# A gated delta-rule layer on one core: two position changes in hand-written engine orders

## What is computed

```python
mixed_qkv = einsum('bsh,ch->bcs', x, Wqkv)          # 2048 q + 2048 k + 4096 v channels
mixed_qkv = silu(causal_depthwise_conv(mixed_qkv, conv_w))   # 4 taps
beta, g = sigmoid(b), -exp(A_log) * softplus(a + dt_bias)
for t in time:                                       # per head, state 128 x 128
    state = state * exp(g_t)
    delta = (v_t - state^T k_t) * beta_t
    state = state + k_t delta^T
    out_t = state^T q_t                              # q, k are l2-normalised
y = (rms_norm(out) * norm_w * silu(z)) @ Wout.T
```

## Time and profile before

| | |
|---|---|
| median of 3 runs | 3998.91 us (3998.87 to 4000.12) |
| the profiled execution's own time | 3996.14 us |
| its span on the core | 3994.4 us |
| mean granted TensorE clock | 0.954 of full speed |
| busy share PE / DVE / ACT / POOL | 87% / 72% / 50% / 23% |
| turns of the delta stage | 64, some 40.4 to 42.8 us each |

### The profile page before, as it was taken

How to read it: one execution, slowest core, us unless ns; L and a number is a source line. 1 busy time by engine, 2 the same in 40 slices (tenths; PEclk the granted TensorE clock), 3 DMA queues, 4 the chain that set the end, 5 groups by cost and what they waited for, 6 DMA issues and landing times. The chain is left out here.

```text
span 3994.4 us, 82462 instructions
## 1 busy us (share of the span) xinstructions
PE 3462.2 (87%) x29419; PEld 2470.9 (62%) x29438; DVE 2876.2 (72%) x5136; ACT 2000.5 (50%) x4971; POOL 927.0 (23%) x1273
## 2 busy tenths in 40 slices
PE   7999977725899999999999999999999999995185
PEld 6888855414566666666666666666666666663142
DVE  3444459984777777777777777777777777775897
ACT  2233320024565666656666565666656666564354
POOL 0000034302223232222323223232232323230000
PEclk9999989867999999999999999999999999997598
DMA  2000021101011000010100101001010110101201
GB/s 100 12 12 6 12 86 34 29 13 53 22 28 34 22 29 23 28 39 17 34 18 28 39 17 34 18 29 38 17 34 18 33 34 17 34 17 43 84 1 43
DMA packets 44453, 122.64 MB, mean 31 GB/s; under 512 B 5872, under 2 KB 11120, under 8 KB 40688
## 3 DMA queue, kind: packets, MB, share of 16 engines
q1 hardware_dynamic: 44016, 116.87, 9.1%
HBM read 112.32 MB, written 4.54 MB: 29 GB/s over the span
## 5 line engine op out<-in xcount | busy, mean ns | idle before, releaser
L1838 DVE SCALAR_TENSOR_TENSOR delta_F<-delta_bank,delta_cw,delta_F 128x510 f32<-128x510 f32 (+2 forms) x768 | 571.4, 744 | 113.4 <-ACT delta_F L1656 94.3
L1846 DVE TENSOR_TENSOR delta_Pb<-delta_bank,delta_lev 128x512 f16<-128x512 f32 x448 | 312.7, 698 | 261.5 <-PE delta_bank L2159 247.4
L2133 PE MATMUL delta_bank<-delta_xh,delta_qkvh 128*128 128x512 f16 x1024 | 391.1, 382 | 20.6 <-DVE delta_F L1838 15.4
L1656 ACT ACTIVATE delta_F<-delta_bank,delta_cw 128x512 f32<-128x512 f32 x256 | 175.9, 687 | 445.9 <-PE delta_bank L2133 445.9
L2133 PE MATMUL delta_bank<-delta_xl,delta_qkvh 128*128 128x512 f16 x1024 | 390.9, 382 | 0.0
L2133 PE MATMUL delta_bank<-delta_xh,delta_qkvl 128*128 128x512 f16 x1024 | 390.2, 381 | 0.0
L1855 DVE CAST delta_XT<-delta_bank 128x512 f16<-128x512 f32 x448 | 309.6, 691 | 43.9 <-PE delta_bank L2182 43.6
L1626 ACT ACTIVATE delta_Xi<-delta_bank 128x512 f16<-128x512 f32 x320 | 190.5, 595 | 192.2 <-PE delta_bank L2178 192.2
L2118 PE MATMUL delta_bank<-delta_zh,delta_xh 128*128 128x256 f16 x1024 | 280.5, 274 | 5.0 <-ACT delta_gz L1678 0.6
L1464 POOL TENSOR_SCALAR_AFFINE_SELECT delta_LA<-delta_LA 128x512 f32<-128x512 f32 x128 | 81.6, 637 | 863.1 <-DVE delta_LA L1866 720.8
L2118 PE MATMUL delta_bank<-delta_zl,delta_xh 128*128 128x256 f16 x1024 | 279.7, 273 | 0.0
(11 more groups left out here) (304 smaller groups left out, 9200.5 us busy)
## 6 DMA issues: line engine op xcount, KB each, us to landing
delta_Gb<-g_rows SPq DMA_DIRECT2D x66, 512.0 KB, 5.2
delta_st_qkv<-in_Wqkv SPq DMA_DIRECT2D x17, 1024.0 KB, 8.4
delta_st_z<-in_Wz SPq DMA_DIRECT2D x17, 512.0 KB, 6.1
conv_T<-filters SPq DMA_DIRECT2D x32, 256.0 KB, 3.1
delta_st_o<-in_Wout SPq DMA_DIRECT2D x16, 512.0 KB, 8.1
ffn_ahead_W<-in_W SPq DMA_DIRECT2D x2, 4096.0 KB, 17.4
conv_ahead_C<-in_ctx_rev SPq DMA_DIRECT2D x1, 6144.0 KB, 17.5
attn_xt<-in_xT SPq DMA_DIRECT2D x10, 512.0 KB, 3.9
```

The source lines that it names most:

```text
L1656: sc.activation(F[:, i, :], bank[AT[job] % 2][:, :], ACT.Copy, scale=cw_tap(i, 3))\
L1838: ve.scalar_tensor_tensor(dst, src, cw_tap(i, 3 - lag), dst, ALU.mult, ALU.add)\
L1846: ve.tensor_tensor(left(Pb[:, lvl, :, :], lvl), comp(bank[5], lvl), bc(lev[:, lvl, :].rearrange("p (n s) -> p n s", s=1 << lvl), 1, 8), AL ...
L2133: ins = te.matmul(bk[:, :], ww[:, QKV[job], kc, :], xx[:, kc, tok:tok + 512], start=(m == 0), stop=(m == 11))
```

## The change

Two edits, both in order only. No instruction is added, removed or altered, and no wait is added or removed. On DVE the two splits of the output weight move down, the first behind `decayed_j0(1)`, the second behind `newton`. On PE `values_token_major(1)` moves from ahead of `fill(5)` to behind it.

```diff
@@ DVE's order @@
                 output_variance()
                 level_xt(4, 0)
                 add_out(3, -2)
-                next_o(0)
-                next_o(1)
                 level_p(5, 0)
                 decayed_j0(1)
+                next_o(0)
                 newton()
+                next_o(1)
                 conv_lag("q", 1, 2, 3)
                 level_xt(5, 0)
                 level_p(6, 0)
@@ PE's order @@
                 level_a(6, 0)
                 fill(4)
                 level_b(6, 0)
+                fill(5)
                 values_token_major(1)
-                fill(5)
                 level_a(0, 1)
                 answer(0, 0)
                 transpose_out(0)
```

## The result

The changed kernel takes 4016.34 us (median of 5 runs, 4015.12 to 4022.99), the kernel before 3998.87 on the same chip (5 runs). The ratio is 1.0049, with a 95% interval of 1.0035 to 1.0063: slower by some 0.5%. The profiled execution took 4015.24 us, 19.1 more than the one before; the medians are 17.5 apart.

What follows compares the result with a forecast made beforehand. The prediction took PE to bound the delta stage, with DVE setting the pace from level_a(5) to z0.0. Four turns cost 3 x 0.34 + 0.20 - 0.09 = 1.13 us, times 15.5 is 17.5: median 4016, range 4003 to 4028.

Steps and rivals of the forecast that it cites:

- z0.0 is pinned behind `conv_lag("k")`: On PE, z0.0 waits for DVE's conv_lag("k") and starts 0.06 to 0.13 us behind its end, whatever PE did before.
- the new wait: PE's idle time gathers at z0.0 as one wait, some 62 times 1.5 us, near 90 us.
- The PE edit costs 0.34 us in three turns and 0.20 in one: times_L(0, 0) on PE starts later behind z0.0: 0.34 us in three turns of four, 0.20 in the other.
- the issue wait: Idle of 0.15 us before the answer in one turn of four; its slack takes 0.14 of the delay, leaving 0.20.
- the transposes': Second pair of value transposes on PE, now behind z0.1: take 0.49 us, so level_a(0) starts 0.49 later.
- ACT's path: conv_tap("v0") to first_answer(0): level with PE's path; if the longer, 0.40 us in place of 0.34, 4 us more in all.
- The DVE edit gains 0.09 us in a split turn: In 16 turns level_p(5) starts 1.42 us earlier, the splits' 1.33 come back before conv_lag("q"): 0.09 gained, between nothing and 0.2.
- Sum: Both edits over four turns: 3 x 0.34 + 0.20 - 0.09 = 1.13 us; 15.5 such groups make 17.5 us.
- the 0.79 wait was the only one: Rival at PE's transposes: level_a(0) comes 0.79 us earlier in each of 62 turns, -49 us, 3950; chance 0.05.
- the delay is taken up later: Rival: slack between times_L and level_a(5) absorbs the delay, no change, 3991 to 4007; chance 0.13.
- The upper bound: Rival: the answer keeps its 0.41 us behind level_a(0), costing 0.49 in all turns, 30 us, 4029; chance 0.08.
- The clock: Rival: long idle before z0.0 lowers PE's clock, 1.5 us each turn, 91 us in all, about 4107; chance 0.02.

Runs made afterwards that it cites:

- out_early: Kernel before, with transpose_out(0) moved on PE from behind the answer to ahead of values_token_major(1): ratio 0.9937.
- z_behind_answer: Kernel before plus the PE edit, with room moved from fill(5) to fill(6) so z0.0 and z0.1 come behind the answer: ratio 1.0028.
- splits_behind_newton: Kernel before, PE's order unchanged, with both output-weight splits moved on DVE behind newton: ratio 1.0017.

## Why the prediction was right, and where it wasn't

The forecast of 4016 met the measured 4016.34, but closer than its terms deserve. Two of them were off, in opposite directions, and the profiled execution grew by 19.1 us, not by the forecast's 17.5; that the medians stand just 17.5 apart is luck within their scatter of several us.

- *z0.0 is pinned behind `conv_lag("k")`.* Right: 0.06 to 0.13 us behind it in all 62 turns of both kernels, and the new wait came as named (62 times, 93.5 us, for "near 90").
- *The PE edit costs 0.34 us in three turns and 0.20 in one.* The mechanism held, the size was high. `times_L` starts 3.77 behind z0.0 in all four kinds of turn now; before, it was 3.51 in two, 3.70 in the kind of the earlier trace rows and 3.44 in the kind ahead of a split turn. So the edit cost 0.27 twice, 0.07 where the issue wait vanished as supposed, and 0.33 in the last kind, which I had not told apart: there z0.0 stands 0.13 behind `conv_lag("k")`, and the answer, which waited for the cast and not for z0.0, stood only 0.57 behind z0.0. Four turns cost 0.94 instead of 1.22. The term that was mis-sized is the transposes': I took 0.49 us from their old place, and behind z0.1 they take 0.43 to 0.44 and are recorded with 0.60 instead of 0.66. Why is open. The missing idle time alone isn't shown to be it: in `out_early` they take 0.49 with no idle time ahead (1812.20 to 1812.69). The shorter group shortens PE's path and ACT's. ACT's `conv_tap("v0")` started at 0.87, only 0.04 behind the recorded end, so the modelled end was not late by the 0.12 that would have made ACT's path the longer one. From the answer to `times_L` PE takes 2.88 us, against 2.87 before, so ACT added nothing that can be seen; with `first_answer(0)` done 0.07 before `times_L`, the two paths came out level, as forecast.
- *The DVE edit gains 0.09 us in a split turn.* Wrong in sign: it lost 0.29, and 5 us alone. The step that failed is "The splits' 1.33 us come back ahead of `conv_lag("q")`, however. What is left is 1.42 - 1.33 = 0.09 us". They came back as 1.33 plus the 0.37 by which `newton` slowed beside POOL, and 1.42 - 1.33 - 0.37 is -0.28. Its slow third operation was in the trace of before, beside POOL's select; I didn't ask what stood beside it on POOL.
- *Sum.* 0.94 + 0.29 = 1.23 us in four turns for the 1.13 of the forecast, and 15.5 times that is the 19.1 of the profiled executions. A match to the tenth is more than this sum can promise, since the issue waits at the loop's seam vary between 1.1 and 1.8 us from one pass to the next.
- *Rivals.* That the 0.79 wait was the only one is refuted by `z_behind_answer` too. That the delay is taken up later is refuted: from `times_L` to the next turn's `decayed_j1` it is 33.37 us before and 33.38 after in ordinary turns. The upper bound, 0.49 in each turn, was not reached: no kind of turn lost more than 0.33. The clock stayed where it was: the granted clock from 1000 to 3600 us is 1.00 (2.4 GHz) in both kernels, with 1.5 us of idle time in each turn.

## What to carry to other kernels

When one engine stands idle for another, follow the other's order beyond the operation that ends the wait: here three more gates stood right behind it, and reordering the waiting engine only moved the idle time and put new work behind the last gate. What helps is independent work from behind the last gate, brought into the idle time, or taking work off the other engine ahead of it. Before moving a DVE operation that has all its inputs in SBUF, look at what POOL does at the new place.

## What the runs showed of the hardware

Where a DVE operation with its inputs in SBUF alone met a POOL operation, one of the two took longer. A split of 128x512 took 0.74 to 0.75 us with POOL idle, 1.18 beside POOL's cast of 0.61, and 1.13 to 1.75 beside POOL's adds; a `newton` operation on 128x8 took 0.16 to 0.17 or 0.55 to 0.60. POOL's select grew from 0.64 to 0.92, its add from 1.27 to 1.71, beside a split. DVE operations that read PSUM kept their time beside POOL (2.31 and 2.30 us for three).

The Trainium skill (SBUF — State Buffer, Who interferes with whom) gives a rule for this: DVE and GpSimd (POOL here) share a port pair under an exclusive lock, and a DVE operation with two SBUF inputs contends with a GpSimd one that reads SBUF, as does a DVE operation in a two-port mode; whichever issues first keeps the pair, and the other blocks. The rows agree on who contends and on the size: `newton`'s L1900, 0.60 from 1735.35, ends 0.02 behind POOL's select (1735.01 + 0.92). They don't show which of the two issued first where both start together: in `splits_behind_newton` the split is recorded 0.03 ahead of the cast, and yet it is the split that pays. Nor do they show a two-port mode; `newton`'s slow L1905 has one tensor input and would need it by the rule. Read with the POOL row of before, the rule would have warned of the sign of the DVE edit.
